# Point-cloud attention in a Trainium2 kernel: ranks counted per tile, three value buffers, whole rows of values, early weights, and another order in ACT's step

## The reference

```
def _sorted_indices(coords_bn3):
    q = _quantize(coords_bn3)                       # 10 bits for each of 3 coordinates
    qt = q[..., jnp.array([1, 0, 2])]
    keys = [_morton_key(q), _morton_key(qt), _hilbert_key(q), _hilbert_key(qt)]
    return [jnp.argsort(kk, axis=1) for kk in keys] # stable: ties by index
...
# for each of two stages, over windows of 10 points along each of the 4 sort orders:
x16 = x.astype(jnp.float16).astype(jnp.float32)     # centre features, neighbour - centre
scores = jnp.einsum('bihd,bjhd->bhij', qh, qh) / np.float32(np.sqrt(headdim))
attn = jax.nn.softmax(scores, axis=-1)
out = jnp.einsum('bhij,bjhd->bihd', attn, qh).reshape(B * N, k, total)
fused = out @ W_lin.T + b_lin
h = _lrelu(_instance_norm(jnp.einsum('oc,bnkc->bonk', W_conv, g), (2, 3)))
feats = h.max(axis=-1)
# then f3 = concat(feats, feats1, feats2), a 1x1 convolution, norm, leaky ReLU
```

## Time and profile before

| | us |
|---|---|
| median of the runs | 1169.45 (1167.97 to 1170.92) |
| profiled execution | 1169.7 |
| its span, first to last instruction | 1167.9 |
| busy in the span: PE, DVE, ACT, POOL | 933.9, 758.2, 460.4, 362.1 |
| end of the sort phase's last instruction | 135.78 |
| attention stages: first POOL instruction | 190.26 and 399.83 |
| convolution's first matmul | 563.61 |

### The profile page before, as it was taken

How to read it: one execution, slowest core, us unless ns; L and a number is a source line. 1 busy time by engine, 2 the same in 40 slices (tenths; PEclk the granted TensorE clock), 3 DMA queues, 4 the chain that set the end, 5 groups by cost and what they waited for, 6 DMA issues and landing times. The chain is left out here.

```text
span 1167.9 us, 26493 instructions
## 1 busy us (share of the span) xinstructions
PE 933.9 (80%) x10400; PEld 665.1 (57%) x10400; DVE 758.2 (65%) x1844; ACT 460.4 (39%) x913; POOL 362.1 (31%) x272
## 2 busy tenths in 40 slices
PE   2892387788869799897389999939987699985898
PEld 1671255556545466676178999937435455552675
DVE  6899997887979488999433232374432389863542
ACT  0899565753327555333012222240002178760100
POOL 0000037998822587885020000000000256520000
PEclk9995597998979899999689999979998799997799
DMA  4773233222233834662044545405526538501000
GB/s 137 292 244 108 62 87 74 36 37 47 38 87 98 142 46 60 87 80 40 9 138 136 159 137 159 138 2 183 147 82 221 214 115 318 192 32 36 1 1 18
DMA packets 156158, 123.70 MB, mean 106 GB/s; under 512 B 52601, under 2 KB 130233, under 8 KB 154514
## 3 DMA queue, kind: packets, MB, share of 16 engines
q1 hardware_dynamic: 155394, 117.97, 38.3%
q10 hardware_dynamic: 656, 4.23, 0.9%
HBM read 109.84 MB, written 12.32 MB: 105 GB/s over the span
## 5 line engine op out<-in xcount | busy, mean ns | idle before, releaser
L568 POOL TENSOR_TENSOR stage_diff<-win_ext,win_F 128x960 f16<-128x960 f32 x88 | 165.5, 1883 | 55.0 <-DVE stage_hi L729 41.7
L1071 ACT ACTIVATE attend_prob<-attend_centred 124x480 f32<-124x480 f32 x88 | 52.3, 594 | 137.1 <-DVE attend_centred L1114 137.1
L1309 DVE TENSOR_SCALAR attn_qT<-proj_qp,attn_bq,attn_gq 128x256 f32 x32 | 17.4, 544 | 122.9 <-ACT attn_sq L1288 122.9
L980 POOL TENSOR_TENSOR attend_pnorm<-attend_prob,attend_inv 124x480 f32<-124x480 f32 x88 | 86.8, 986 | 24.6 <-DVE attend_inv L1127 24.3
L369 ACT ACTIVATE sort_signs<-sort_keysB,sort_key 128x512 bf16<-128x512 f32 x120 | 84.8, 714 | 18.4 <-DMA sort_keysB<-scratch_keys 18.4
L1107 DVE TENSOR_REDUCE attend_top<-attend_score 124x32 f32<-124x480 f32 x88 | 56.1, 638 | 49.4 <-PE attend_score L1014 49.0
L1042 PE MATMUL attend_outp<-stage_FX,stage_WX 128*64 128x240 f32 (+3 forms) x352 | 75.7, 395 | 6.6 <-DMA stage_vT<-scratch_values 6.6
L1014 PEld LDWEIGHTS attend_score<-stage_hi,stage_diff 128*60 128x60 f16 x1376 | 49.6, 114 | 29.6 <-issue 23.9
L1261 PE MATMUL proj_qp<-core_xnT,attn_wq 128*128 128x256 f32 x256 | 63.5, 392 | 2.3 <-DMA attn_wv<-in_Wv_dram 1.8
L1026 PE MATMUL attend_prob_t<-core_ident,attend_pnorm 124*128 124x124 f32 x344 | 57.9, 291 | 9.3 <-POOL attend_pnorm L980 7.9
L1725 PE MATMUL cross_score<-cross_kT,cross_qblock 128*128 128x512 f32 x128 | 61.8, 608 | 3.2 <-POOL cross_qblock L1806 2.6
(11 more groups left out here) (328 smaller groups left out, 2202.8 us busy)
## 6 DMA issues: line engine op xcount, KB each, us to landing
binary_base<-in_fmean_dram SPq DMA_DIRECT2D x8, 1344.0 KB, 8.6
cross_raw<-in_fw_dram SPq DMA_DIRECT2D x24, 448.0 KB, 7.0
sort_ctxT<-in_ctxT_dram SPq DMA_DIRECT2D x8, 1024.0 KB, 7.0
attn_wq<-in_Wq_dram SPq DMA_DIRECT2D x32, 256.0 KB, 2.9
attn_wk<-in_Wk_dram SPq DMA_DIRECT2D x32, 256.0 KB, 3.3
attn_wv<-in_Wv_dram SPq DMA_DIRECT2D x32, 256.0 KB, 3.7
att_wo<-in_Wo_dram SPq DMA_DIRECT2D x32, 256.0 KB, 2.7
stage_vT<-scratch_values SPq DMA_DIRECT2D x64, 120.0 KB, 5.5
```

Of the source, the lines that this page charges most:

```text
L568: return nc.gpsimd.tensor_tensor(out[:, :, 0:size], spread, f.unsqueeze(3).to_broadcast([P, QB, size, WIN]), ALU.subtract)
L980: nc.gpsimd.tensor_tensor(pnorm[g % 2][:, 0:n, 0:K].rearrange("p r (h w) -> p r h w", w=SPAN), prob[g % 3][:, 0:n * HEADS].rearrange("p (r ...
```

## The change

Five things change.

1. **Ranks.** ACT's sign passes leave out the tile itself: a pass over the later tiles against a slightly smaller bound (`keyDown`), and one over the earlier tiles against a slightly larger bound (`keyUp`), which settles ties by the tile's position. DVE makes the bounds (`make_bounds`) and compares each tile only with itself, 128 wide. In methods 1 to 3 the last tile is counted by DVE over 384 keys. PE's tie matmuls are gone.
2. **Values of stage 0** are laid out as in stage 1: 8 DMAs a part, pieces twice as long, and two matmuls over 64 rows in place of one over 128. Both write the same PSUM tile.
3. **`VRING`** is 3 instead of 2, in both stages.
4. **The convolution's weights** are requested by SP at the start of stage 1's attention.
5. **ACT's step** in attention has `second_half` ahead of `exponent`.

```diff
+                    if b == 0:
+                        act.wait_ge(bounds, 1 if m < METHODS // 2 else 2)
...
                     for t in range(signed_tiles(m)):
-                        if last_use[t]:
-                            act.wait_ge(signed, last_use[t])
                         at = row * KC + t
-                        nc.scalar.activation(signs[t][:], keysB[:, row * N:(row + 1) * N], ACT.Sign, scale=-1.0,
-                                             bias=key[:].bitcast(F32)[:, at:at + 1], accum_out=order[:, row:row + 1, t]).then_inc(signed, 1)
+                        for side, (limit, first, end) in enumerate(((keyUp, 0, t), (keyDown, t + 1, KC))):
+                            if first == end:
+                                continue
+                            u = count % KC
+                            if last_use[u]:
+                                act.wait_ge(signed, last_use[u])
+                            nc.scalar.activation(signs[u][:, 0:(end - first) * P], keysB[:, row * N + first * P:row * N + end * P], ACT.Sign,
+                                                 scale=-1.0, bias=limit[:, at:at + 1],
+                                                 accum_out=order[:, side, row:row + 1, t]).then_inc(signed, 1)
...
+                def make_bounds(h):
+                    cols = slice(h * HALF, (h + 1) * HALF)
+                    dve.wait_ge(key_ready, h + 1)
+                    go(vec.tensor_scalar(keyOut[:, cols], key[:, cols], 1, None, ALU.bitwise_or))
+                    go(vec.tensor_scalar(keyUp[:, cols], key[:, cols].bitcast(F32), 1.0 - 2.0 ** -24, None, ALU.mult))
+                    away = keyOut[:, cols].bitcast(F32)
+                    go(vec.tensor_tensor(keyDown[:, cols], keyUp[:, cols], away, ALU.min))
+                    vec.tensor_tensor(keyUp[:, cols], keyUp[:, cols], away, ALU.max).then_inc(bounds, 1)
...
-                        vec.scalar_tensor_tensor(out=equals[b][t][:], in0=keysB[:, row * N:row * N + (t + 1) * P],
-                                                 scalar=keyF[:, at:at + 1], in1=earlier[:, (KC - 1 - t) * P:N], op0=ALU.is_equal,
-                                                 op1=ALU.mult, accum_out=ties[:, row:row + 1, t]).then_inc(tied, 1)
+                        vec.scalar_tensor_tensor(out=own[compares % KC][:], in0=keysB[:, row * N + t * P:row * N + (t + 1) * P],
+                                                 scalar=keyF[:, at:at + 1], in1=earlier[:], op0=ALU.subtract, op1=ALU.is_lt,
+                                                 accum_out=inner[:, row:row + 1, t]).then_inc(compared, 1)
...
-VRING = 2
+VRING = 3
...
+                if beside:
+                    beside(sp)
...
-                                if G == 1:
-                                    mm = nc.tensor.matmul(made[0][pair * 2 * O:(pair + 1) * 2 * O, cols], vT[part % VRING][:, x, pair, :],
-                                                          probT[u][:, y:y + SROWS], start=False, stop=True, skip_group_check=True)
-                                    continue
                                 for a in range(2):
                                     rows = slice(a * STEP, (a + 1) * STEP)
-                                    mm = nc.tensor.matmul(made[a][pair * O:(pair + 1) * O, cols], vT[part % VRING][rows, x, pair, :],
+                                    dst = made[0][(pair * 2 + a) * O:(pair * 2 + a + 1) * O] if G == 1 else made[a][pair * O:(pair + 1) * O]
+                                    mm = nc.tensor.matmul(dst[:, cols], vT[part % VRING][rows, x, pair, :],
                                                           probT[u][rows, y:y + SROWS], start=False, stop=True, skip_group_check=True)
...
-                ticks((TURN_LAG, bring), (SCORE_LAG, exponent), (TURN_LAG, second_half))
+                ticks((TURN_LAG, bring), (TURN_LAG, second_half), (SCORE_LAG, exponent))
```

More of the change, by code:

```diff
@@ L336, in _ @@
                 mm.then_inc(low_turned, 1)
-                def count_later(row):
-                    pe.wait_ge(tied, (row + 1) * KC)
-                    for s0 in range(KC - 1):
-                        for t in range(s0 + 1, KC):
-                            mm = nc.tensor.matmul(laterP[:, s0, row:row + 1], equals[row % B][t][:, s0 * P:(s0 + 1) * P], one[:],
-                                                  start=(t == s0 + 1), stop=(t == KC - 1))
-                    mm.then_inc(eq_used, 1)
                 turn_keys(0)
@@ L457, in _ @@
                 keyF = key[:].bitcast(F32)
+                make_bounds(1)
+                dve.wait_ge(bounds, 2)
                 dve.wait_ge(earlier_ready, 1)
-                go(vec.memset(one[:], 1.0))
+                compares = counts = 0
                 for row in range(METHODS * B):
@@ L474, in _ @@
-                    if signed_tiles(m) < KC:
-                        if b >= 2:
-                            dve.wait_ge(counted, b - 1)
-                        vec.tensor_scalar(below[b % 2][:], keysB[:, row * N:(row + 1) * N], keyF[:, at:at + 1], None, ALU.is_lt, ALU.add,
-                                          accum_out=order[:, row:row + 1, KC - 1]).then_inc(counted, 1)
-                dve.wait_ge(tied, METHODS * B * KC)
-                dve.wait_ge(signed, sum(B * signed_tiles(m) for m in range(METHODS)))
@@ new lines, in _ @@
+                        compares += 1
+                        if t >= signed_tiles(m):
+                            if counts >= KC:
+                                dve.wait_ge(counted, counts - KC + 1)
+                            vec.tensor_scalar(below[counts % KC][:, 0:t * P], keysB[:, row * N:row * N + t * P], keyUp[:, at:at + 1], None,
+                                              ALU.is_lt, ALU.add, accum_out=order[:, 0, row:row + 1, t]).then_inc(counted, 1)
+                            counts += 1
@@ new lines, in _ @@
+                dve.wait_ge(compared, compares)
+                dve.wait_ge(counted, counts)
+                go(vec.tensor_scalar(order[:, 0, B:, KC - 1:KC], order[:, 0, B:, KC - 1:KC], 2.0, -float(N - P), ALU.mult, ALU.add))
+                dve.wait_ge(signed, sum(B * (2 * signed_tiles(m) - 1 - (signed_tiles(m) == KC)) for m in range(METHODS)))
+                go(vec.tensor_tensor(order[:, 0], order[:, 0], order[:, 1], ALU.add))
+                go(vec.tensor_scalar(order[:, 0], order[:, 0], float(N - P), 0.5, ALU.add, ALU.mult))
@@ L492 @@
+                go(vec.tensor_tensor(T["rank"][:].rearrange("p (a t) -> p a t", t=KC), order[:, 0], inner[:], ALU.add))
 BLK = 12
```

120 lines of the change are left out of this document (55 added, 65 removed).

## The result

The changed kernel takes 1142.45 us (median of 4 runs, 1139.34 to 1144.25) beside 1170.18 for the kernel before in the same comparison. The ratio is 0.9755, with a 95% interval of 0.9718 to 0.9793. The prediction was 1147, with a range of 1140 to 1157. The profiled execution took 1143.61 us; its span fell from 1167.9 to 1141.9, 26.0 less.

A forecast was written before the change was run, and what follows sets the result against it. DVE was taken to bound the sort, POOL stage 0's second half and DVE undisturbed stage 1; 7.7 + 4.0 + 4.0 + 3.3 + 1.2 + 2.2 = 22.4 off 1169.7 gave 1147 us, range 1140 to 1157.

The forecast's parts named there:

- Sort, ACT: End of the sort phase: cheaper sign passes on ACT bring the rank at 127.7 against 135.78, 7.7 us gained.
- rival C: ACT's sort passes: narrow sign passes cost what wide ones do, 9.8 us lost instead of 7.7 gained, 1165; chance 0.05.
- Sort, DVE: DVE's compare loop in the sort phase: starts near 72.5 and ends at the latest at 124.7 us.
- Attention, scaled copies: ACT's step in both attention stages: scaled copies moved ahead of the exponential, 4.0 us gained in each stage.
- Rival B: ACT in attention: reordering yields nothing, the exponential now being late; the 8.0 us stay, 1155; chance 0.11.
- Values, three buffers: Value loads at each second half of attention: PE's waits go, 3.3 us gained in stage 0, 1.2 in stage 1.
- Values, the matmuls: Stage 0's value matmuls in attention: 32 on half the rows and columns replace 16 at nil cost.
- Rivals A and D: Stage 0's value matmuls: A, row halves take turns, 1155 us, 0.12; D, each waits for the other's drain, 1257, 0.03.
- The convolution: Start of the last convolution: its weights come during stage 1, so PE's first matmul gains 2.2 us.
- Arrange: Arrange phases: fewer SP requests and a third buffer cleared on an idle POOL, counted as nothing.
- The sum: Whole kernel: all gains together 22.4 us, from 1169.7 to 1147.3.

The follow-up runs named there:

- the second profile: The changed kernel, unedited, profiled again in a later comparison beside the kernel before: 1140.82 us, ratio 0.9794.

## Why the prediction was right, point by point

**Sort, ACT.** The step that failed is "It comes some 0.6 us earlier", of the last evacuation. In the profiled run it came 2.4 us later than before, at 90.44. PE's chain starts behind the turning of the keys, and these come some 1 us later, four small DVE instructions; I let ACT's later start vanish in waits for PE but forgot that PE's own start moves too. Besides, PE waited 1.03 and 0.51 us for late context loads. From there my sum holds: 90.44 + 1.0 + 16 x 2.35 = 129.0. In the second profile PE had neither late load, and its first eight context matmuls behind a wait took 3.70 us where they had taken 5.40 before and in the first; the evacuation came at 87.06. With the old sort phase and the same 3.70 it came at 86.02, with the new one and 3.70 at 86.18 to 87.06 in five profiles: at equal terms 0.2 to 1.0 later and not 0.6 earlier. That the rank came at 126.70 there, against 127.7 predicted, is partly luck: the shorter matmuls outweighed the step that failed. Over the eight profiles the rank gained 5.7 to 9.95 us, and 7.7 lies within. Two slips change nothing: 135.78 - 127.7 is 8.1 and not 7.7, and 80 x 0.70, in rival C's condition, is 56.0 and not 56.3.

**Sort, DVE.** The loop was to end by 124.7 at the latest; it ended at 120.3. The own compares cost 0.27 and the 384-element counts 0.54, where I had taken 0.67 as the bound.

**Attention, scaled copies.** Right in mechanism; the 8.0 predicted for both stages came out as 8.5 by the order alone in the kernel before, and 8 to 13 by its removal. In stage 0 the profiles show it, 4.4 to 6.7 us, and ticks of 2.80. In stage 1 it shows in the undisturbed ticks, 3.06 beside 3.32, and is covered by PE's stands in the whole stretch. Rival B falls with the exponential that still waits for DVE.

**Values, three buffers.** The waits went, as predicted, but not by the cause that the step leads with. In stage 0 either the third buffer or the halved transfers is enough, and only in stage 1 does the third buffer remove a wait, 2.39 us. Against that stands its clearing, which holds up DVE: 0.8 us ahead of stage 0 and 1.6 to 2.1 ahead of stage 1. The two cancel about, as the equal times with two and three buffers have it. Its use is another: it lets the transfers be paced.

**Values, the matmuls.** Nil, as predicted: 0.62 us for 32 beside 0.68 for 16, and 115.85 and 114.95 us of attention with the new form, 114.97 with the old. Rivals A and D fall. The Trainium skill, "PSUM — Partial Sum Buffer", section "PSUM bank collisions raise a hardware error", quotes that different row tiles can't access a bank at the same time; read as turns that made 1.17 us in the prediction's estimate, and the trace's 0.62 disagrees. It fits the same section's other sentence, that a different quadrant of the same bank does not collide, which stands there for two engines.

**The convolution** gave 2.6 instead of 2.2: the 0.4 that I left for the entry of the block was not needed.

**Rival C** falls with the passes of 0.38, 0.49 and 0.60 us.

**Arrange.** The second step that failed is "a third buffer is cleared on an idle POOL. I count nothing". POOL is idle there, but DVE is not, and it loses about what the clearing takes. In stage 0 the narrower buffers make up for the third one: DVE's 16 comparisons beside it fell from 8.43 to 7.49 us, which is the 0.8 gained between the rank and the first tick. In stage 1, where the width stays, they grew from 8.43 to 10.06. SP's eight fewer requests are worth nothing that the traces show.

**The sum.** 22.4 predicted, 26.0 in the spans, and 24 to 29 by the two ratios. The forecast was 67% and came in. The undershoot of 3.6 is made of 2.1 behind the convolution's start, 1.6 in the stretch of stage 1, 0.8 ahead of stage 0's first tick, 0.7 in its attention and 0.4 at the convolution, less the 2.0 that the sort gave too little. The first two are not to be read as gains of the change: the phases behind the convolution's start, with the same code in all 14 profiles, took 597.5 to 605.6 us. For the same reason the losses by ratio of the kernels with one part taken back don't add up: they come to more than the whole gain.

## What to carry to other kernels

When a bound moves to another engine, follow that engine's chain back through every engine it waits for: here four small DVE instructions on the path to PE moved ACT's end by up to 1.0 us, where ACT's own later start cost nothing that shows. A wait that two edits each remove is to be credited to neither before one of them is tried alone. Work put on an engine that idles is not free for its neighbours: look at how long the other engines' instructions beside it take. Where an engine stops inside a group and nothing releases it, look at the DMA share just before: spread large transfers over the time that a spare buffer gives.

## What the runs showed of the hardware

Bursts of DMA stop PE with nothing in the profile to wait for: up to 3.05 us for a burst of eight 120 KB transfers, up to 4.75 with twice the bursts, and PE's clock was at its lower level after the longer ones (0.59 and 0.50 granted in the 3 us behind them). The same stretch of one kernel took 216.36 and 221.31 us in two executions, with 2.8 and 5.4 us of such stands in stage 1's attention. DVE's comparisons of 512 elements (bf16 out, f16 in) took up to 1.97 us instead of 0.34 while POOL cleared a buffer beside them; four clearings of 2.02 to 5.61 us in sum made DVE's 16 take 6.73 to 10.05 us instead of 4.28. Thirty-two matmuls of 64 rows by 32 columns on four column strips and two row halves, all into one PSUM tile, took 0.62 us. ACT's sign pass with a sum cost 0.38, 0.49, 0.60 and 0.70 us from start to start for 128, 256, 384 and 512 elements, a fixed 0.28 and 0.10 to 0.11 for each 128. The first eight context matmuls behind a wait for DMA took 5.40 us in some executions and 3.70 in others (clock granted over them: 0.68 and 1.00), at about the same wait (1.92 to 3.25 and 2.19 to 3.09 us), so whether the clock falls in such a wait is not told by its length.
